# Gated cross-attention with a ternary feed-forward: first slots with work of VectorE given to ScalarE and GpSimd, and the closing part's downs laid between the last up pieces

## What is computed

```python
def layernorm(x): return (x - mean(x)) / sqrt(var(x) + 1e-5)

q = rms_norm(layernorm(x) @ q_w.T + q_b) * norm_q          # 16 heads of 32
k = rms_norm(ctx @ k_img_w.T + k_img_b) * norm_k_img        # the 128 context rows are all image rows
v = ctx @ v_img_w.T + v_img_b
a = softmax(q @ k.T / sqrt(32)) @ v
x1 = x + tanh(g_xattn) * (a @ o_w.T + o_b)

w1, w2 = ternary(W_fc), ternary(W_proj)                      # groups of 64: sign(w) * scale where |w| is over half of it
h = square(relu(layernorm(x1) @ w1.T))                       # 2048 wide
out = x1 + tanh(g_ffn) * rms_norm(h) @ w2.T
```

## Time and profile before

| what | value |
|---|---|
| median of three runs | 1010.25 us |
| the profiled execution | 1009.37 us |
| its span, first to last instruction | 1007.6 us |
| TensorE matmul busy | 930.6 us (92%) |
| VectorE busy | 690.1 us (68%) |
| ScalarE busy | 717.9 us (71%) |
| GpSimd busy | 566.1 us (56%) |
| mean granted clock of TensorE | 0.97 |

### The profile page before, as it was taken

The page is one execution under the profiler, slowest core; times in us unless marked ns, Lnnn a source line. Parts: engine busy times, 40 slices in busy tenths (PEclk is TensorE's granted clock), DMA queues, the critical chain, the costliest instruction groups (busy, mean ns, idle before and its releaser), DMA issues.

```text
span 1007.6 us, 26077 instructions
## 1 busy us (share of the span) xinstructions
PE 930.6 (92%) x9942; PEld 570.9 (57%) x10043; DVE 690.1 (68%) x1360; ACT 717.9 (71%) x1235; POOL 566.1 (56%) x616
## 2 busy tenths in 40 slices
PE   4776597899999999999999999999999999999997
PEld 1343354566665656666666565666666665656663
DVE  7898987777677677767767676767677776766200
ACT  2777767678777777777877777777787777777653
POOL 1223334665656565767656565657666566656655
PEclk9797798999999999999999999999999999999999
DMA  8735431333333344343323334433343423232200
GB/s 302 182 82 149 107 91 43 75 75 75 74 71 68 75 85 86 85 75 75 81 69 75 70 72 80 86 85 75 78 81 68 79 69 72 55 64 54 43 21 21
DMA packets 184588, 82.43 MB, mean 82 GB/s; under 512 B 170000, under 2 KB 170000, under 8 KB 182928
## 3 DMA queue, kind: packets, MB, share of 16 engines
q1 hardware_dynamic: 184464, 80.77, 36.1%
HBM read 30.67 MB, written 8.39 MB: 39 GB/s over the span
## 4 chain that ended last, share of the span: by engine, by line
PE 78%; issue 7%; ACT 4%; DVE 3%; POOL 2%; DVEq 0%; POOLq 0%; ACTq 0%
PE mix_ps L440 10%; PE up_pair L426 10%; PE up_pair L427 9%; PE mix_ps L439 8%; PE score_ps L397 7%; PE score_ps L396 7%; PE score_ps L395 7%; PE tr_a L395 2%; PE tr_a L397 2%; PE tr_a L396 2%; PE score_ps L510 2%; PE score_ps L487 2%; PE mix_ps L577 1%; PE tr_a L440 1%; PE up_pair L449 1%
## 5 line engine op out<-in xcount | busy, mean ns | idle before, releaser
L426 PE MATMUL up_pair<-ft,w 128*128 128x256 f16 x960 | 217.1, 274 | 1.2 <-ACT h_sb L791 1.2
L427 PE MATMUL up_pair<-ft,w 128*128 128x256 f16 x960 | 217.1, 275 | 0.0
L440 PE MATMUL mix_ps<-w,big 128*128 128x512 bf16 x464 | 176.1, 380 | 10.0 <-issue 8.6
L1628 POOL TENSOR_TENSOR k_weighted<-k_raw,qk_norm 128x512 f32<-128x512 f32 x32 | 41.9, 1310 | 253.6 <-DVE k_raw L1157 252.1
L1642 POOL TENSOR_TENSOR big<-h_sb,big 128x512 f16<-128x512 f32 x128 | 155.0, 1211 | 14.8 <-ACT big L797 8.7
L1652 POOL TENSOR_TENSOR hh_sum<-hh_sum,hh_sb 128x512 f32<-128x512 f32 x112 | 154.3, 1378 | 4.9 <-ACT hh_sb L813 4.9
L439 PE MATMUL mix_ps<-w,big 128*128 128x512 bf16 x382 | 145.1, 380 | 2.9 <-POOL big L1642 2.9
L862 ACT ACTIVATE score_ps<-score_ps,log_p,exp_scale 128x512 f32<-128x512 f32 x128 | 95.7, 748 | 58.7 <-PE score_ps L513 58.7
L1069 DVE TENSOR_TENSOR p_lo<-score_ps,p_hi 128x512 f16<-128x512 f32 x128 | 88.1, 689 | 47.4 <-ACT p_hi L744 47.0
L791 ACT ACTIVATE h_sb<-up_pair,relu_scale 128x512 f32<-128x512 f32 x120 | 81.3, 678 | 36.9 <-PE up_pair L427 36.3
L426 PEld LDWEIGHTS up_pair<-ft,w 128*128 128x128 bf16 x960 | 94.4, 98 | 19.4 <-ACT h_sb L791 1.9
(11 more groups left out here) (223 smaller groups left out, 2327.9 us busy)
## 6 DMA issues: line engine op xcount, KB each, us to landing
x_sb<-in_x SPq DMA_DIRECT2D x32, 256.0 KB, 3.0
ctx_sb<-in_ctx_t SPq DMA_DIRECT2D x32, 256.0 KB, 2.7
out<-out_sb SPq DMA_DIRECT2D x32, 256.0 KB, 2.0
big<-in_w_fc_t SPq DMA_DIRECT2D x4, 1024.0 KB, 5.3
big<-in_w_proj_t SPq DMA_DIRECT2D x4, 1024.0 KB, 5.1
big<-in_wq_t SPq DMA_DIRECT2D x1, 1024.0 KB, 7.1
big<-in_wk_t SPq DMA_DIRECT2D x1, 1024.0 KB, 9.2
big<-in_wv_t SPq DMA_DIRECT2D x1, 1024.0 KB, 10.2
```

The source lines that it names most:

```text
L426: nc.tensor.matmul(dst[:, half], w, ft[i][:, c, :], start=(c == 0), stop=False)
L427: last = nc.tensor.matmul(dst[:, half], w, ft[i][:, C + c, :], start=False, stop=(c == C - 1))
L440: last = nc.tensor.matmul(dst[:, :], ht_lo[i][:, row], w2[:, m, :], start=False, stop=(m == M - 1))
```

## The change

- Statistics: `row_stats` keeps its first two operations. GpSimd's `norm_rows` scales the variance itself (a new operation of one column) and subtracts the mean. `context_scale` keeps step and reciprocal; the two scales become one GpSimd operation of two columns, `unscales(t)`, behind `hidden_gain` in its list, and `k_out` and `x1_out` wait for it.
- Context scale of tiles 2 to 6: ScalarE sums the absolute values (`context_total`) instead of VectorE's maximum, and the spread is an fp32 product. Weight scales of q and v: ScalarE's `weight_sum` instead of VectorE's `weight_max`.
- Ternary halves n = 22 to 31: ScalarE copies them (`raw_half`), four in slot 3 and six in slot 4 (before six and four), and VectorE clips whole pairs in SBUF. TensorE waits for the copies, no longer for clips. Mask and products of pair 15 move into slot 5.
- Warms: 10 become 6 in slots 1 and 2, with 8 and 6 new ones at their ends; 12 become 6 in slots 3 and 4.
- The closing part: order of the downs and up pieces below; the last eight pieces use three banks in turn instead of four.

```diff
 def context_total(t, par):                       # new, ScalarE
+    act.wait_ge(ctx_in[par], 16 * (t // 2 + 1))
+    act.wait_ge(ctx_spread, t)
+    act.wait_ge(qss_ready, t)
+    nc.scalar.activation(square_out[:, :], ctx_sb[par][:, :], ACT.Abs, accum_out=ctx_sum[:, :]).then_inc(ctx_part_ready, 1)
 def raw_half(n):                                 # new, ScalarE
+    p = n // 2
+    act.wait_ge(gsum_done, n + 1)
+    need(act, tsigned_ready, p - TD + 1)
+    copy_hi(t_scale[p % TD][:, n % 2 * 512:(n % 2 + 1) * 512], up_b, raw_ready)
 def unscales(t):                                 # new, GpSimd
+    if t == 1:
+        pool.wait_ge(setup_dve, 2)
+    pool.wait_ge(ctx_step_ready, t + 1)
+    need(pool, kraw_ready, t - 2)
+    need(pool, x1_ready, t - 2)
+    nc.gpsimd.tensor_tensor(unscale[t % 3][:, :], ctx_step[:, :].to_broadcast([P, 2]), unit_scale[:, :],
+                            ALU.mult).then_inc(unscale_ready, 1)
 def row_stats(src, raw, mv, done, n):            # VectorE
     nc.vector.bn_stats(raw[:, :], src).then_inc(done, 1)
     nc.vector.bn_aggr(mv[:, :], raw[:, :]).then_inc(done, 1)
-    nc.vector.tensor_scalar(pair[:, 0:1], mv[:, 0:1], -1.0, None, ALU.mult).then_inc(done, 1)
-    nc.vector.tensor_scalar(pair[:, 1:2], mv[:, 1:2], LN_EPS, X_SCALE ** -2, ALU.add, ALU.mult).then_inc(done, 1)
 def norm_rows(...):                              # GpSimd
+    nc.gpsimd.tensor_scalar(var[:, :], mv[:, 1:2], LN_EPS, X_SCALE ** -2, ALU.add, ALU.mult).then_inc(rstd_ready, 1)
 ...
 # VectorE, middle_slot(t), behind the tops
-    ternary_products(p - 1); ternary_half(n) ... ternary_half(n + 5)
+    ternary_final(p - 1) ... ternary_clip(p); ternary_mask(p); q_out(t + 1); k_lo(t + 1) ... ternary_clip(p + 1)
 # TensorE, slot(t)
-    ffn_up(g, j, 3, up_ps)
+    if more:
+        ffn_up(g, j, 3, up_ps)
     pe.wait_ge(attn_ready, 2 * t + 2)
-    ffn_down(s + 1 - LAG, range(0, 4), mix_ps)
+    ffn_down(s + 1 - LAG, range(0, 4 if more else 16), mix_ps)
+    if not more:
+        project_out(t)
+        ffn_up(g, j, 3, up_ps)
 # TensorE, closing_slot
-    ffn_down(NT - 1 - LAG, range(4, 16), mix_ps)
-    project_out(NT - 1)
     ffn_up(g, j, 0, up_b)
+    ffn_up(g, j, 1, up_ps)
     ffn_down(NT - LAG, range(0, 4), k_ps)
-    ffn_up(g, j, 1, up_ps)
+    ffn_up(g, j, 2, up_b)
     ffn_down(NT - LAG, range(4, 8), k_ps)
-    ffn_up(g, j, 2, up_b)
     ffn_up(g, j, 3, up_ps)
-    ffn_down(NT - LAG, range(8, 12), k_ps)
+def last_piece(n):
+    ffn_up(NG, n // UP, n % UP, score_ps[1 + n % 3], 3)
 # TensorE, behind closing_slot
+    last_piece(0)
+    ffn_down(NT - LAG, range(8, 12), k_ps)
+    last_piece(1)
     ffn_down(NT - LAG, range(12, 16), k_ps)
+    square_sums(NT - LAG)
     pe.wait_ge(x1_ready, NT)
-    ffn_down(NT - 3, range(0, 8), tr_a)
-    square_sums(NT - LAG)
-    ffn_down(NT - 3, range(8, 16), tr_a)
-    pe.wait_ge(out_ready, NT - 3)
-    for j in range(2):
-        for f in range(UP):
-            ffn_up(NG, j, f, score_ps[f], 4)
+    for n in range(2, 6):
+        last_piece(n)
+        ffn_down(NT - 3, range(4 * n - 8, 4 * n - 4), tr_a)
+    last_piece(6)
+    last_piece(7)
+    pe.wait_ge(out_ready, NT - LAG)
```

More of the change, by code:

```diff
@@ L128, in gated_cross_attention_kernel @@
         ctx_top = sb("ctx_top", [P, 1])
-        ctx_top0 = sb("ctx_top0", [P, 1])
+        ctx_sum = sb("ctx_sum", [P, 1])
+        ctx_step0 = sb("ctx_step0", [P, 1])
         ctx_step = sb("ctx_step", [P, 1])
         ctx_scale = sb("ctx_scale", [P, 1])
-        k_unscale = sb("k_unscale", [P, 1])
-        o_unscale = [sb(f"o_unscale_t{i}", [P, 1]) for i in range(3)]
+        unscale = [sb(f"unscale{i}", [P, 2]) for i in range(3)]
         ct_hi = sb("ct_hi", [P, D], F16)
@@ L572, in next_context @@
                 pe.wait_ge(ctx_part_ready, t + 3)
-                spread(tr_a, ctx_part[:, :], ctx_spread, ident_b)
+                if t <= J:
+                    spread(tr_a, ctx_sum[:, :], ctx_spread)
+                else:
+                    spread(tr_a, ctx_part[:, :], ctx_spread, ident_b)
             def warm(n):
@@ L908, in first_slot @@
                 q_hi(1)
+                context_total(2, 0)
                 attention_hi(0)
@@ L933, in early_slot @@
                 q_hi(t + 1)
+                context_total(t + 2, t % 2)
                 ternary_abs(p + 3)
@@ L1156, in k_out @@
                 need(dve, klo_ready, t)
-                nc.vector.scalar_tensor_tensor(out=k_raw[:, :], in0=k_ps[:, :], scalar=k_unscale[:, :], in1=kb_sb[:, :],
+                dve.wait_ge(unscale_ready, t + 1)
+                nc.vector.scalar_tensor_tensor(out=k_raw[:, :], in0=k_ps[:, :], scalar=unscale[t % 3][:, 0:1], in1=kb_sb[:, :],
                                                op0=ALU.mult, op1=ALU.add).then_inc(kraw_ready, 1)
@@ L1300, in output_constants @@
                 chain(nc.vector.tensor_tensor(tmp_c[:, 0:1], w_step[:, 2:3], w_step[:, 3:4], ALU.mult))
-                chain(nc.vector.tensor_scalar(o_unscale0[:, :], tmp_c[:, 0:1], gain[:, 0:1], 1.0 / (V_SCALE * C_MAX), ALU.mult,
-                                              ALU.mult))
-                chain(output_scale(0, ctx_top0))
+                chain(nc.vector.tensor_scalar(unit_scale[:, 1:2], tmp_c[:, 0:1], gain[:, 0:1], 1.0 / V_SCALE, ALU.mult, ALU.mult))
+                nc.vector.tensor_tensor(unscale[0][:, 1:2], ctx_step0[:, :], unit_scale[:, 1:2], ALU.mult).then_inc(setup_dve, 1)
             def constant_row():
```

177 lines of the change are left out of this document (89 added, 88 removed).

## The result

| | before | after |
|---|---|---|
| median | 1009.72 us (4 runs, 1007.72 to 1010.44) | 1027.95 us (4 runs, 1027.15 to 1031.07) |
| profiled execution, span | 1007.6 us | 1029.2 us |
| VectorE, ScalarE, GpSimd busy | 690.1, 717.9, 566.1 us | 633.4, 727.0, 681.5 us |

A forecast was written before the change was run, and what follows sets the result against it. TensorE was taken to bound the steady slots, VectorE and hand-overs the early ones, ScalarE the closing part. Gains of 1.5 + 2.5 + 4.7 + 0 + 7.7 = 16.4 us gave 993.8 us, range 988 to 1000.

The forecast's parts named there:

- What bounds the kernel now: Whole kernel: TensorE bounds 249 to 946 us; gains lie before 193 us (VectorE, hand-overs) and after 930 us (ScalarE).
- Slots 5 to 30: zero: Steady slots: GpSimd's three added small operations cost nothing, hidden in waits or within 1.35 us of slack before q's transpose.
- Rival (c): Steady slots: GpSimd's additions pass q's slack, 1.3 us a slot over 26 slots, 35 us slower, 1029 us; chance 0.04.
- Opening: 1.5: Before the first scores: two weight reductions moved from VectorE to ScalarE gain 1.5 us, bounds 0.5 and 2.3.
- Slots 0 to 2: 2.5: Slots 0 to 2: less VectorE work and fewer warms gain 2.5 us, bounds 1 and 6.
- Slots 3 and 4: 4.7: Slots 3 and 4: half clips leaving VectorE, earlier ctx_part and fewer warms gain net 4.7 us, bounds -1 and 9.
- Rival (a): Slots 3 and 4: ScalarE becomes the bound and the gain there is nothing, 998.5 us; chance 0.12.
- Slot 5: Slot 5: pair 15's moved mask and products lie in waits; its tops come 0.8 us later in relation.
- Closing: 7.7: Closing part: the new order of downs and up pieces gives TensorE back net 7.7 us, bounds 5 and 8.7.

The follow-up runs named there:

- e4: Before, with only the closing part of the change: 1002.42 us, ratio to before 0.9921.
- e5: e1 with the variance step and both unscales back on VectorE: 1002.19 us, ratio to before 0.9911.
- e1: After, with GpSimd's normalising operations adding the mean negated by VectorE instead of subtracting the mean: 1006.43 us, ratio to before 0.9963.
- e2: Before, with GpSimd's normalising operations subtracting the mean instead of adding its negative: 1029.64 us, ratio to before 1.0194.
- e8: e4 with the weight reductions of q and v as sums on ScalarE (the opening alone): 1001.69 us.
- e7: e5 with slot 5's down blocks 12 to 15 behind the output projection, pair 14's products and pair 15's clip behind the near tops: 997.75 us, ratio 0.9866.
- e9: e7 with the ten ternary half clips of slots 3 and 4 back on VectorE in place of ScalarE's copies: 993.58 us, ratio to before 0.9838.
- e11: e7 with two more ScalarE passes of 0.63 us in each of slots 3 and 4, behind the context sum: 1000.9 us in a single run.
- e10: e7 with twelve warms instead of six in slots 3 and 4: 994.95 us in a single run.
- e13: e9 with twelve warms instead of six in slots 3 and 4: 993.30 us, ratio to before 0.9832.

## Why the prediction was wrong, step by step

**The sum of the change, from medians.** Before to e4, closing part: -8.2. e4 to e5, opening, slots 0 to 5 and what VectorE lost in the steady slots: -0.2. e5 to e1, small operations to GpSimd: +4.2. e1 to after, subtract for add: +21.5. Together +17.3, measured +18.2. The -0.2 hides larger parts, as told under e5: in the profiles 5.0 us lost in slot 5 and 5.6 won elsewhere.

**What bounds the kernel now.** That the steady slots are TensorE's, and that VectorE's relief buys nothing there, held: e5, whose VectorE has less to do, has odd slots of 27.99 against 28.13. What was not drawn from it: such a stretch can hardly get shorter by work moved between the other engines, only longer. There the price of each operation put on another engine has to be known. One reading was off: the 11.4 us for `v_lo` stand ahead of the scores at 63.4, 89.9 and 120.8, at the ends of slots 0 to 2, and not in slots 3 and 4. There TensorE waited 5.0 us for `t_scale`, 4.7 for `ctx_part` and 3.1 for `abs_w`.

**Slots 5 to 30: zero.** This is the step that failed. It counted what GpSimd gained as three small operations and passed over the one whose form changed: the subtraction was taken at the price of the addition, 0.77 us, with no row for it. It measured 2.08 us. An operation that the trace doesn't show needs bounds; the nearest row of before, an addition of two tiles, would have set one at some 0.6 us a call more, 1.2 a slot:

```profile
L1676 POOL TENSOR_TENSOR xb<-x_sb,o_const 128x512 f32<-128x512 f32 x32 | 42.9, 1341 | 0.0
```

e2 shows that the subtraction alone is worth 19 us. The second error is the slack. The additions were held against q's transpose, but the low halves and the sums of the hidden pieces at the list's end were tighter: e1's waits for `hh_sum`, 2.2 us in 11 slots, and 0.53 us in each odd slot from operations of 0.19 to 0.34 us.

**Rival (c)** gave 1029 us, and 1028 were measured. It named the right engine, but its mechanism was not the one at work: q's transpose was late once, by 0.5 us, the price was put on small operations, and all 26 slots were to grow by 1.3, where twelve grew by 1.55. With the 9.1 us that after had lost up to slot 6 and the 6.4 that the closing part won, the agreement is chance.

**Opening: 1.5.** The first scores came 1.76 us earlier in after (1.3 to 2.6 in the experiments that have the new opening). The size was right. That it is kept to the end is not shown: e8 is 0.7 us faster than e4, with intervals that overlap.

**Slots 0 to 2: 2.5.** In after they are 3.9 us longer; with the addition back (e1, e5, e7, e9) 0.5 to 1.2 shorter than before. So the subtraction cost 4.4 us here too (e1), and the term itself was mis-sized by half or more. TensorE's waits for `v_lo` did shrink, from 11.4 us to 8.1 in e5, but its busy time in these slots rose from 57.9 to 62.8 us (the new warms are in it), so a shorter wait was not a shorter slot. What each step is worth there was not tried.

**Slots 3 and 4: 4.7.** The sum of this term has a price for ScalarE and for waits, but none for TensorE's clock, and that is where most of it went. With the ten copies on ScalarE the two slots of e5 and e7 gain 0.4 and 0.6 us on before; e1, with the same copies, gains 4.4. The stretch from `scores_t` to the end of the output projection took 3.77 us twice in before, 5.54 and 5.61 in e5: 3.6 us for the lower clock. Rival (a) has the right number for e5 and e7 (a gain of nothing) and only a part of the reason: the copies cost about 2 us by the estimate under e9, and e11 shows that ScalarE's work behind the context sum comes back in full. Nor did VectorE win what was taken from it, since the clips and masks in SBUF ran long beside GpSimd. The near tops of slot 4 did leave earlier (7.5 us after the scores in e5, 10.2 in before), but at the end of the output projection only 0.5 of these 2.7 us were left (14.3 against 14.75), and the second half of the slot took these too. Some 4.2 us, nearly the term, appear in e9, with the copies undone and a part of the clock back, and in e1, with the copies and most of the clock. So the size of the term could be reached, and what it needed beside VectorE's relief was a clock that the prediction took for granted.

**Slot 5.** The mask and products of pair 15 were said to lie in waits, and only 0.8 us was charged for the clip ahead of the tops. In fact the near tops began 3.8 us behind the scores in place of 1.65, and the first down waited 1.40 us for pair 15 ahead of `scores_t`, which no step of the prediction had: 5 us in e5, 6.5 in after. Of these, 0.9 and 2.4 us are the lower clock from `scores_t` to the end of the projection (5.45 and 6.95 us against 4.57 in before). The early slots' gain was work put off, and slot 5 paid for it; e7 gets it back with a better place.

**Closing: 7.7.** Right: 8.2 by e4's median (6.8 to 9.2 by the interval), 7.1 in the profile. The first relu of the last pieces stands 42.2 us behind slot 31's scores (960.25 in e4; 53.7 in before), and the clock is 1.00, as forecast. That TensorE would have no wait over 1 us did not come: it waits once for x1's transpose, 1.8 us in e4 where 0.7 was estimated, and 0.3 in e10 and e13 with the same closing part.

The best kernel of the study is e13, 993.3 us, 1.7% faster than before and no different from e9: the change without the subtraction, without GpSimd's small operations and without the copies on ScalarE, with the last pairs later in slot 5 and twelve warms in slots 3 and 4. It is at the forecast of 993.8, by other parts than the forecast had.

## What to carry to other kernels

An edit that moves an operation and rewrites its arithmetic on the way is two edits; the rewritten form needs a row or a probe of its own before it is given the old price. Where an engine's list has idle time at its head, look at its tail for the slack: what is queued last before the bound's next need decides. And a gain in early slots counts only if the work moved out of them finds real room where it lands: look at the first slot after the last one that was relieved. Before a difference between two kernels is put down to an engine, hold one stretch of the same TensorE work in both against its granted clock: here 3.0 us between e1 and e5 in slots 3 and 4 lay there.
